# Causal mask of the last attention layer: from a matmul ahead of every head's scores to GpSimd selects after the exponential

## The reference, cut to what matters

```python
latent = x @ Wc_down
q = (latent @ Wq_up).reshape(Bsz, Tlen, N_HEAD, HEAD_DIM)
kv = latent @ Wkv_up
k, v = (kv[..., :HEAD_DIM], kv[..., HEAD_DIM:])
att = jnp.einsum('bthd,bsd->bhts', q, k) * scale
att = jnp.where(causal[None, None], att, -jnp.inf)
att = jax.nn.softmax(att, axis=-1)
y = jnp.einsum('bhts,bsd->bthd', att, v).reshape(Bsz, Tlen, C)
return y @ Wc_proj
```

## Time and profile before

| | before |
|---|---|
| median of 3 runs | 1881.12 us (1879.36 to 1881.54) |
| the profiled execution, own time | 1879.98 us |
| its span | 1878.1 us |
| busy over the span: TensorE, VectorE, ScalarE, GpSimd | 1303.5, 1278.6, 775.8, 420.3 us |
| the L3_ATTN stage | about 1475 to 1685 us of the span |
| mean granted clock of TensorE over the execution | 0.828 of full speed |

### The profile page before, as it was taken

One profiled execution on the slowest core, in us unless ns is written; L12 is line 12 of the kernel. 1 busy time (PEld: TensorE's weight loads), 2 busy tenths in 40 slices (PEclk: granted clock), 3 DMA queues, 4 the chain that ended last, 5 costly groups with the idle time before them and its releaser, 6 DMA issues.

```text
span 1878.1 us, 28508 instructions
## 1 busy us (share of the span) xinstructions
PE 1303.5 (69%) x8838; PEld 900.0 (48%) x8838; DVE 1278.6 (68%) x3333; ACT 775.8 (41%) x1332; POOL 420.3 (22%) x628
## 2 busy tenths in 40 slices
PE   2665657999767776557766665466666699976776
PEld 2544545888633333443333332355555444445665
DVE  5989987666666674556666565777877466647776
ACT  3343352333336665534444443233333156643333
POOL 3335342000133230112222222222221122200000
PEclk8887888999859888866777777687877699988998
DMA  6000000000000000000000000000000000000000
GB/s 254 0 0 0 0 0 1 0 0 0 0 1 1 0 1 1 0 1 1 0 0 0 0 0 1 1 1 0 0 0 0 0 2 1 1 1 1 0 0 22
DMA packets 5657, 13.66 MB, mean 7 GB/s; under 512 B 225, under 2 KB 4449, under 8 KB 5089
## 3 DMA queue, kind: packets, MB, share of 16 engines
q1 hardware_dynamic: 5600, 12.96, 1.8%
HBM read 11.91 MB, written 1.05 MB: 7 GB/s over the span
## 4 chain that ended last, share of the span: by engine, by line
issue 59%; PE 10%; DVE 9%; POOL 7%; POOLq 6%; DVEq 4%; ACT 3%; ACTq 2%
DVEq L1563 3%; DVE sbuf L1562 2%; POOL w_l0f L431 2%; POOLq L430 2%; PE PS L901 2%; PE PS L976 1%; POOLq L356 1%; PE PS L924 1%; POOL trs L357 1%; PE PS L918 1%; POOL PT L324 1%; PE PS L882 1%; POOL hrs L357 1%; POOL PT L317 1%; ACTq L535 1%
## 5 line engine op out<-in xcount | busy, mean ns | idle before, releaser
L1641 DVE TENSOR_REDUCE mx<-PS 128x2 f32<-128x512 f32 (+1 forms) x256 | 156.0, 620 | 83.5 <-PE PS L924 74.9
L602 ACT ACTIVATE w_l0f<-PS 128x512 f32<-128x512 f32 (+1 forms) x256 | 136.7, 543 | 104.7 <-PE PS L931 102.5
L355 POOL TENSOR_TENSOR tve<-tmv,eps 128x2 f32<-128x2 f32 x64 | 12.5, 195 | 741.2 <-DVE tmv L1427 739.0
L755 ACT ACTIVATE sg<-PS 128x512 f32<-128x512 f32 (+1 forms) x104 | 60.3, 580 | 202.3 <-PE PS L1338 202.0
L1144 PE MATMUL PS<-w_l0f,VA 128*32 128x256 f32 (+1 forms) x1024 | 88.5, 523 | 62.7 <-POOL w_l0f L431 48.4
L667 ACT ACTIVATE w_l0f<-PS,one_c 128x384 f32<-128x384 f32 x128 | 75.4, 589 | 134.1 <-PE PS L1132 133.4
L1338 PE MATMUL PS<-hT,w_l0f 128*128 128x256 f32 x512 | 122.4, 385 | 0.0
L850 PE MATMUL PS<-cb,w_const 128*128 128x256 f32 x128 | 43.8, 474 | 99.5 <-DVE sbuf L1567 99.4
L2074 DVE TENSOR_TENSOR y<-sg,PS 128x512 f32<-128x512 f32 (+1 forms) x104 | 69.2, 666 | 59.8 <-ACT sg L755 47.2
L1338 PEld LDWEIGHTS PS<-hT,w_l0f 128*128 128x128 f32 x512 | 94.9, 194 | 11.0
L1773 DVE SCALAR_TENSOR_TENSOR w_l0f<-w_l0f 128x384 f32<-128x384 f32 x128 | 77.6, 615 | 31.9 <-ACT w_l0f L667 27.1
(11 more groups left out here) (362 smaller groups left out, 3509.4 us busy)
## 6 DMA issues: line engine op xcount, KB each, us to landing
w_l0f<-in_l0f SPq DMA_DIRECT2D x1, 3076.0 KB, 13.8
w_l2f<-in_l2f SPq DMA_DIRECT2D x1, 2214.0 KB, 19.8
w_l3f<-in_l3f SPq DMA_DIRECT2D x1, 1736.0 KB, 23.4
w_l0a<-in_l0a SPq DMA_DIRECT2D x1, 1093.0 KB, 7.5
result<-X SPq DMA_DIRECT2D x1, 896.0 KB, 4.6
X<-in_x SPq DMA_DIRECT2D x1, 768.0 KB, 9.7
w_l1f<-in_l1f SPq DMA_DIRECT2D x1, 582.0 KB, 15.5
PT<-in_cbf SPq DMA_DIRECT2D x1, 576.0 KB, 10.6
```

The lines of the kernel that those rows point to most:

```text
L602: act.activation(P8[:, hh % 8, 0:width], PS[:, hh % 2, 0:width], ACT.Exp, scale=SM_SCALE).then_inc(a["pt"], 1)
L1641: dve.tensor_reduce(mx[:, hh, 0:nm], PS[:, 2 + hh % 2, 0:nm * keys].rearrange("p (t k) -> p t k", t=nm), AX.X, ALU.max).then_inc(a["mx"], 1)
```

## The change

"mask_k" is no longer multiplied in; the scores of the weights start their own accumulation and are exponentiated unmasked. After each exponentiated head GpSimd runs one `affine_select` over the two diagonal blocks of its slot (2 x 128 f32 on each of 128 partitions), which keeps elements with query at or after key and writes 0.0 to the others. A new semaphore `sel` counts them, and `values` waits for it in L3_ATTN. "mask_q" stays. GpSimd's `one` is written out over k, with its former work at k = 0, 2, 4, 5 and 8 and a select at each k: heads 3 to 15 of unit i and heads 0 to 2 of unit i + 1. In L3_ATTN TensorE's `outputs_transpose`, `outputs_back`, `project_out` and the four `values` move one step later, as does ScalarE's `outputs_copy`. L1_ATTN keeps its order.

```diff
@@ -223,7 +223,7 @@

         AT = {l: {n: sem(f"t{l}_{n}") for n in (own + " qkv tr m st pt pv ot otr o oT oTs").split()}
               for l, own in ((L1_ATTN, "ld ks qs kq va pl s mx mtr mev"), (L2_ATTN, "split eva evd pn pg"),
-                             (L3_ATTN, "ld ks qs kq va pl s mx mtr mev lat lats"))}
+                             (L3_ATTN, "sel ld ks qs kq va pl s mx mtr mev lat lats"))}

         FF = {l: {n: sem(f"f{l}_{n}") for n in ("gate ge gx g y o oc " + own).split()}
               for l, own in ((L0_FFN, "hn sg"), (L1_FFN, "hn"), (L2_FFN, "c rk"), (L3_FFN, "hn sg cn c cT"))}
@@ -402,21 +402,37 @@
                         pool.tensor_copy(VAs[par][:, :, 0:nk, 0:HD],
                                          vfs[par][:, 0:T * nk].rearrange("p (t a) d -> p t a d", t=T)).then_inc(a["va"], 1)

+                    def causal_part(u, hh):
+
+                        pool.wait_ge(a["pt"], u * NH + (hh + 1))
+                        pool.sem_inc(a["pl"], 1)
+                        own = P8[:, hh % 8, 0:2 * L].rearrange("p (t q) -> p t q", t=T)[:, :, 0:P]
+                        pool.affine_select(own, own, pattern=[[0, T], [1, P]], compare_op=ALU.is_ge, fill=0.0, base=0,
+                                           channel_multiplier=-1).then_inc(a["sel"], 1)
+
                     def one(i, par):
-                        if within(i, 1):
-                            values_for(i + 1, 1 - par)
-                        if within(i, 2):
-                            pool.wait_ge(a["ld"], (i + 3) * LOADS[l])
-                            pool.wait_ge(a["tr"], (i + 2) * COPIES[l])
-                            pool.sem_inc(a["pl"], 1)
-                            split_keys(pool, l)
-                            head_rstd(i + (head0[l] + 4))
-                            if not isinstance(i, int) or i >= 0:
-                                pool.wait_ge(a["mtr"], 2 * i + 2)
-                            pool.sem_inc(a["pl"], 1)
-                            split_queries(pool, l, par)
-                        if within(i, -1):
-                            tail_rstd(i + tail0[l])
+                        A, M, B, D_ = within(i, 0), within(i, 1), within(i, 2), within(i, -1)
+                        for k in range(NH):
+                            if k == 0 and M:
+                                values_for(i + 1, 1 - par)
+                            if k == 2 and B:
+                                pool.wait_ge(a["ld"], (i + 3) * LOADS[l])
+                                pool.wait_ge(a["tr"], (i + 2) * COPIES[l])
+                                pool.sem_inc(a["pl"], 1)
+                                split_keys(pool, l)
+                            if k == 4 and B:
+                                head_rstd(i + (head0[l] + 4))
+                            if k == 5 and B:
+                                if not isinstance(i, int) or i >= 0:
+                                    pool.wait_ge(a["mtr"], 2 * i + 2)
+                                pool.sem_inc(a["pl"], 1)
+                                split_queries(pool, l, par)
+                            if k == 8 and D_:
+                                tail_rstd(i + tail0[l])
+                            if l == L3_ATTN and k < NH - AHEAD and A:
+                                causal_part(i, k + AHEAD)
+                            if l == L3_ATTN and k >= NH - AHEAD and M:
+                                causal_part(i + 1, k - (NH - AHEAD))

                     head_rstd(head0[l] + 2)
                     iterations(pool, one)
@@ -614,7 +630,7 @@
                                 weigh(i + 1, k - (NH - AHEAD))
                             if k == 2 and A:
                                 maxima_copy(i, 1, par)
-                            if k == 3 and D:
+                            if k == (4 if l == L3_ATTN else 3) and D:
                                 outputs_copy(i - 1)
                             if k == 6 and B and l == L1_ATTN:
                                 parts_copy(i + 2, 0, KTs[par][:, lo])
@@ -877,6 +893,7 @@
                     name = {L1_ATTN: "l1a", L3_ATTN: "l3a"}[l]
                     causal = l == L3_ATTN
                     ntr, half, rows = COPIES[l], NH // 4, PARTS + AUG
+                    late = 1 if causal else 0

                     def project(u, t, bank=7):
                         ins = pe.matmul(PS[:, bank, 0:3 * D], hT[:, t * P:(t + 1) * P], w(name, "wqkv"),
@@ -930,8 +947,7 @@
                         q0 = P if causal and t == 1 else 0
                         return pe.matmul(PS[:, b, t * L:(t + 1) * L - q0],
                                          KTs[par][r:r + rows, 0 if causal else hh // 2, t * P:(t + 1) * P],
-                                         QTs[par][r:r + rows, hh // 2, q0:L],
-                                         start=not causal, stop=True, skip_group_check=causal)
+                                         QTs[par][r:r + rows, hh // 2, q0:L], start=True, stop=True)

                     def step(i, k, par, for_maximum, u, hh, upar):

@@ -950,8 +966,6 @@
                                 pe.wait_ge(a["mev"], u * 2 + (1 + hh // (NH // 2)))
                             if not isinstance(u, int) or u > 0 or hh >= 2:
                                 pe.wait_ge(a["pt"], u * NH + (hh - 1))
-                            if causal:
-                                score_mask(hh % 2, "mask_k")
                         for t in range(T):
                             if for_maximum:
                                 ins = max_block(k, t, 1 - par)
@@ -963,7 +977,7 @@
                                     ins.then_inc(a["st"], 1)

                     def values(u, g, par):
-                        pe.wait_ge(a["pt"], u * NH + (g + 1) * HG)
+                        pe.wait_ge(a["sel" if causal else "pt"], u * NH + (g + 1) * HG)
                         if g == 0:
                             pe.wait_ge(a["va"], u + 1)
                             if not isinstance(u, int) or u > 0:
@@ -1009,7 +1023,7 @@
                                 step(i, k, par, M, i + 1, k - (NH - AHEAD) if M else None, 1 - par)

 
-                            if k == 0 and D:
+                            if k == late and D:
                                 outputs_transpose(i - 1)
                             if k == 0 and B:
                                 pe.wait_ge(hd_hT, i + (head0[l] + 3))
@@ -1031,13 +1045,13 @@
                                     pe.wait_ge(a["kq"], NB * ntr)
                                     pe.wait_ge(a["mev"], 2 * i + 1)
                                 maxima_transpose(i, 1, par)
-                            if k == 3 and D:
+                            if k == 3 + late and D:
                                 outputs_back(i - 1)
-                            if k == 3 and A:
+                            if k == 3 + late and A:
                                 values(i, 0, par)
-                            if k == 4 and D:
+                            if k == 4 + late and D:
                                 project_out(i - 1)
-                            if k == 6 and A:
+                            if k == 6 + late and A:
                                 values(i, 1, par)
                             if k == 6 and B and l == L1_ATTN:
                                 if A:
@@ -1056,7 +1070,7 @@
                             if k == 9 and B:
                                 pe.wait_ge(a["kq"], (i + 2) * ntr + (ntr - 2))
                                 head_transpose(l, i + 2)
-                            if k == 10 and A:
+                            if k == 10 + late and A:
                                 values(i, 2, par)
                             if k == 11 and M:
                                 if B:
@@ -1067,7 +1081,7 @@
                             if k == 13 and B:
                                 pe.wait_ge(a["mev"], 2 * i + 3)
                                 keys_transpose(i + 2, range(half, 2 * half) if l == L1_ATTN else range(1))
-                            if k == 14 and A:
+                            if k == 14 + late and A:
                                 values(i, 3, par)
                             if k == 15 and B:
                                 pe.wait_ge(a["kq"], (i + 2) * ntr + (ntr - 1))
```

## The result

The changed kernel takes 1882.5 us (median of 20 runs, 1880.9 to 1886.7) against 1880.1 for the kernel before (20 runs, 1877.2 to 1883.7). The ratio is 1.0016, 95% interval 1.0009 to 1.0024: about 3 us slower. The interval excludes no change at all, but the difference is under the 0.2% that the prediction called the same. The forecast was 1886 in a range of 1870 to 1901.

What follows compares the result with a forecast made beforehand. TensorE was taken as close to the bound, with GpSimd's query path almost without slack. 6 x (-0.1 + 1.1 + 0.3) = +7.8, less 2.7, gave +5.1 us on 1881.1: 1886 us, range 1870 to 1901.

Steps and rivals of the forecast that it cites:

- rival A: GpSimd's chain takes TensorE's place in the attention unit and the clock falls a little; 1882 to 1893 us, chance 0.43.
- What bounds it: Masked attention stage: TensorE close to the bound, busy 20.3 of 22.5 us a unit; GpSimd's query path has next to no slack.
- Removed: TensorE loses 16 masks a unit at 0.16 us each: at most 2.56 us a unit, a step becoming 0.53.
- The select: GpSimd gets 16 selects a unit, 0.43 + 0.12 = 0.55 us each, with 0.40 and 1.10 as ends.
- C: The select on GpSimd is dear, 1.10 + 0.12 us, delaying the query chain; 1902 us, chance 0.15.
- The loop: One unit written out from step 15 at full clock: 22.4 us against 22.5, so a gain of about 0.1 a unit.
- the 13 to 15 that the prediction named as a sign: GpSimd busy 13 to 15 us a unit would show the prediction right.
- The clock: TensorE's granted clock falls through a lull after step 8, costing 1.1 us a unit in six iterations.
- Contention: VectorE's operations reading SBUF slow down while GpSimd is busy: 0.3 us a unit, between 0 and 0.77.
- The sum: Six iterations of -0.1 + 1.1 + 0.3 give +7.8, less 2.7 for the end iterations: +5.1 us.
- B: The TensorE time is really kept, the query chain being off the path and the clock at 1.00; 1871 us, chance 0.27.
- D: Gains and losses cancel, with the clock at 1.00 and no contention; 1878 to 1884 us, chance 0.15.

Runs made afterwards that it cites:

- e4_filler: Changed kernel plus eight extra matmuls, result overwritten, in TensorE's wait ahead of the query transposes; 1872.3 us, ratio 0.9949 to the kernel before.
- e6_neither_old_order: Kernel before without the masks of the weights and without selects, order of before, that causal mask left out; 1877.6 us, ratio 0.9989.
- e7_outT0_filler: Changed kernel with output transposes back at step 0 and eight filler matmuls ahead of the query transposes; 1867.7 us, ratio 0.9929.
- e8_selects_old_order: Changed kernel, selects kept, with the whole order of before (late = 0, ScalarE's outputs_copy at k = 3); 1885.0 us, ratio 1.0025.
- e5_outT0: Changed kernel with only the eight output transposes moved back to step 0; 1878.3 us, ratio 0.9995.
- e1_neither: Changed kernel without its selects, so neither masks of the weights nor selects, new order kept; 1872.4 us, ratio 0.9952.
- e2_order_only: Changed kernel with the masks put back and no selects, so the new order alone; 1875.9 us, ratio 0.9979.
- e3_both: Changed kernel with the masks put back, so masks and selects both in the new order; 1882.0 us, ratio 1.0007.
- e9_short_selects: Changed kernel with eight filler matmuls ahead of the query transposes and selects over 2 x 16 elements instead of 2 x 128; 1868.8 us, ratio 0.9944.
- e12_filler_down: Changed kernel with six filler matmuls ahead of project_down and none ahead of the query transposes; 1883.3 us, ratio 1.0012.

## Why the prediction was right, and where it was not

The result is right in direction and within the range, with rival A's mechanism. Two things in it are luck, and are said below: terms that miss in opposite directions, and a size that lies where the prediction gave the smaller chance.

**What bounds it.** Right. The query chain through GpSimd, with no slack before, became the path. It now ends the largest wait of TensorE (waits of 1535 to 1625 us, changed kernel and then e4_filler):

```profile
PE PS L918 <- POOLq L307: 6.9, 4, 1.9
...
PEld PS L990 <- POOL w_l0f L410: 0.2, 1, 0.2
```

```profile
PEld PS L918 <- POOLq L307: 2.5, 4, 0.8
...
PE PS L918 <- POOLq L307: 0.9, 4, 0.4
```

**Removed.** 0.16 us a mask and 0.53 a step hold (1560.51 to 1561.04). That the 2.56 us would shrink to little holds too: 0.4 is left at full clock, and without any selects e6_neither_old_order keeps 1.1.

**The select.** Sized at 0.43 and measured at 0.41, and two in a row start 0.36 to 0.39 apart instead of 0.55: a little too dear. C, the dear select, is out. The row that it was nearest to, the one-input copy of 256 elements at 0.40, was the right neighbour; no cost of the index comparison shows beside it.

**The loop.** 22.4 us at full clock forecast, 22.1 measured, and both waits to within 0.1 us. Its pieces hold too: from the start of step 15 (1552.95) project_up ends after 6.35 us (forecast 6.25), split_keys starts after 7.2 (7.3), and the query transposes start after 15.3 (15.5). What it had wrong is what the new order costs. The text says that the hole ahead of project_down is written in the order, and so it is, but the order also gives something back. e4_filler against e7_outT0_filler prices the later output transposes at 0.93 us a unit (21.82 against 20.89, both at 1.00). e8_selects_old_order against e5_outT0 prices the later value products and projection at 0.7 us a unit the other way, and without selects e6 and e1 take the same 21.4 at full clock with the old order and the new. With the masks in (e2_order_only) the order is free in the steady units and a gain at the end. The sentence that the value products wait for no select in steady units is borne out: in the 90 us of these rows such waits come to 0.2 us. GpSimd is busy 12.5 us a unit, just under the 13 to 15 that the prediction named as a sign.

**The clock.** The right step, and the one trusted least, but too small. Granted 0.86 in the fallen units; 24.04 against 22.09 is 1.9 us a fallen unit, and the windows show four fallen of five measured (i = 0 to 4), where the text took 1.1 in all six. e4_filler shows that it is the clock and not GpSimd's delay alone: the same selects, the same chain, clock 1.00, 21.8 us. By the ratios the filler is worth 12.6 us over the stage, more than the 6.6 forecast for the clock. By the windows, 12.0 us in all, 8.3 of it lie in the units i = 0 to 4, and the rest in the first iteration (20.6 against 22.5 us) and at the end (60.1 against 62.0), where the filler also raises the clock.

**Contention.** Forecast 0.3 us a unit; slow casts are there, but not by the cause that was forecast, and they cost nothing that shows. The casts of the earlier trace rows in the changed kernel, and two casts of one unit; beside the first stands the L306 above (1590.96, 1.09 us).

```profile
L1667 DVE CAST QS<-mx x8: 206/612/965, 1498.3 to 1650.5; 128x16 bf16<-128x16 f32 x8
```

```profile
1591.15 0.96 DVE L1667 CAST QS<-mx 128x16 bf16<-128x16 f32 x1
...
1592.45 0.40 DVE L1671 CAST QS<-mx 128x16 bf16<-128x16 f32 x1
```

The median of 0.61 lies between two kinds and no cast takes it. Seven of the line's sixteen casts take 0.96 us, where one did before, and each of the seven starts 0.19 us after GpSimd has started the last operation of the split (L306) and ends 0.06 us after it. So it is not a select that holds them: the longer chain has moved the split under this cast. The next cast (L1671) meets a select in six of sixteen times and then takes 0.35 to 0.41 us instead of 0.20. The Trainium skill (GPSIMD Engine Reference, Key points) names VectorE's two-port modes and two-input operations as those that contend with GpSimd. The trace agrees that VectorE is held; these casts have one input, and whether they run in such a mode no view here shows.

None of it is seen in the time of a unit. e3_both against e2_order_only is 0.40 us (22.90 against 22.50) and e4_filler against e1_neither 0.38 (21.82 against 21.44), all at 1.00, and that is the length of the one select on the path (0.41), half of which e9_short_selects takes back. The 0.65 of the changed kernel's own unit at full clock has 0.2 us more, a gap in GpSimd's queue that the three units after it don't have and whose cause is not known:

```profile
1538.99 0.22 POOL L288 CAST KS<-kf 128x48 bf16<-128x48 f32 x1 [0.33 <-issue]
```

**The sum.** Forecast +5.1, measured +2.2 in the stage and +3 by the ratio. The first iteration gave -1.07 (23.54 to 22.47), as worked out, though in e2_order_only the same 1.1 us came with the masks in, at a clock of 0.56 against 0.51. The five whole units i = 0 to 4 gave +6.3, or 1.26 each, where 1.3 was forecast. That agreement is luck: the loop gave -0.45 where -0.1 was counted, contention nothing where 0.3 was, and the clock, averaged over the five, 1.7 where 1.1 was. The rest, from the last project_down on, holds the sixth unit and the iterations 6 and 7, and so 1.3 - 1.3 - 0.4 = -0.4 in the forecast; it gave -3.0. This is the whole difference, and e2_order_only shows that 2.1 of it come from the order and not from the masks: a gain that the sum does not have.

**The rivals.** A it is, with its size at the lower edge. The difference of 3 us counts as the same by the prediction's own line of 3.8 us, to which it gave 0.27, and only 0.07 of that for A; to slower by more it gave 0.46. B is out: TensorE waits for the split in every unit, and even with masks and selects both gone (e6) 1.1 of the 2.56 us are kept. C is out by the select's 0.41 us. D's number would fit the time, but its mechanism, a clock that stays at 1.00, is not what happened. Open is why the unit i = 1 keeps 1.00 in this execution while its neighbours do not; e1_neither shows the same alternation, and e6_neither_old_order a mixture, with shorter lulls.

## What to carry to other kernels

Work taken off the busiest engine is worth what it leaves on the path at the clock that remains: here 128 matmuls were also what kept TensorE's clock up through a wait, and without them most units lost 1.9 us against one that kept it. Write out the loop of one iteration before such a move and look for a second path without slack; here it ran through GpSimd, where one more operation of 0.41 us counted in full. Run a change of order that rides along by itself, part by part: here one part cost 0.9 us a unit, the other gave about 0.7 back, and the best version keeps only the second.

## What the runs showed of the hardware

The granted clock followed the lull after step 8: six extra matmuls elsewhere in the unit (e12_filler_down) left it at 0.86, eight in the lull (e4_filler) kept it at 1.00. Adding 1.4 us of useless matmuls a unit took 10 us off the kernel. A GpSimd select of 256 f32 a partition takes 0.41 us, as much as a plain copy of 256 (0.40), and one of 32 takes 0.21. A VectorE cast of 16 elements that started 0.19 us after a GpSimd operation of 1.1 us took 0.96 us instead of 0.20 and ended 0.06 us after it, seven times of seven in the changed kernel.
